# A two-layer cross-attention and expert kernel on one core: the tiles of the first expert layer that run inside the last routing chain are all put behind it

## The chip, the core and the metric

One Trainium2 chip, one of its cores, one launch. The time is microseconds (us) of device time for the whole program; lower is better. The kernel is written against the engines directly: PE (matrix multiply, with a separate row PEld for its weight loads), DVE (VectorE), ACT (ScalarE), POOL (GpSimd) and SP (SyncE, which only issues DMAs here). Each engine runs its own instruction list in the order in which it was written, and the engines wait for each other on semaphores.

## What is computed

The input is 32 batches of 128 tokens of width 128. There are two layers, each of an attention over a context and an expert network, each added to the residual:

```python
x = x + _L0_xattn_ref(_layernorm(x), ctx_768, mask, Wq, Wkv)        # 16 heads of width 8
x = x + _L0_ffn_ref(_layernorm(x), router_w, router_b, w1, b1, w2, b2)
x = x + _L1_xattn_ref(_layernorm(x), ctx_768, w_q, w_k, w_v, w_out, b_out)   # 16 heads of width 64
x = x + _L1_ffn_ref(_layernorm(x), w_router, gate_up_proj, down_proj, ...)
```

The part that matters here is the first expert network. Every token chooses its best 2 of 8 experts, and each expert takes its first 1280 arrivals in the order of the tokens:

```python
logits = xf @ router_w + router_b
topk_p, topk_i = jax.lax.top_k(softmax(logits), 2)
...                                  # rank = place of the choice inside its expert
keep = rank < cap                    # cap = 1280
buf = zeros(E * cap + 1, d).at[slot].set(xf[st])
h = gelu(einsum('ecd,edf->ecf', buf, w1) + b1)
eo = einsum('ecf,efd->ecd', h, w2) + b2
out = zeros_like(xf).at[st].add(eo_flat[slot] * w)
```

## The kernel before

**First attention.** A batch of 128 tokens is one step; four batches form a quad, and there are eight quads (0 to 7). At a quad's end its normalised rows are transposed on PE (`rows_across`, L1010, tile `gu` in, bank `of` out), copied by ACT (`take_rows`, L1499), multiplied by the router weights (`logits_front`, L960) and copied by ACT (`take_logits`, L1486). DVE picks the two best experts with a chain of small operations (`first_choice`, `second_choice`, L1771 to L1782, result `selq`). PE counts the choices (`rank_front`, L977 to L987), DVE turns the counts into row numbers (`choose_slots`, L1797 to L1806, result `slots`), and POOL scatters the quad's normalised rows into the buffer `buf` in HBM with indirect DMAs, two for each batch, so eight for a quad (`scatter_front`, L714). POOL issues them in order, and the same engine does the roots of the layer norm (`rstd_second`, L691 to L697) and one power at the end (L754).

**Tiles of the first expert network.** The buffer is worked off in 71 tiles of 128 rows (T0 to T70), expert by expert in a table that DVE makes from the counts. The first 33 (T0 to T32, `TA = 33`) hold rows of the first five quads only; their part of the table is ready before the attention ends (`list_tiles(0)`). The other 38 need the last ranks, the last scatters and the second part of the table (`cells_across(1)` on PE, L995, then `list_tiles(1)` on DVE, L1836 to L1847). The step for one tile, spread over four `body(t)` calls, is:

- SP fetches its 64 KB from `buf` into a ring of six (`fetch_tile`, L611), at most six tiles ahead of PE, and stores results with a lag of ten tiles (`store_tile`, L619). At T33 SP first writes the stores up to tile 26, then fetches.
- DVE copies the expert's first weights beside it (`stage_first`, L2235, two tiles ahead).
- PE transposes it (L1346), two tiles later makes the hidden part (L1353), four tiles later the output (L1363). ACT copies the transpose (L1660) and applies Gelu (L1666). DVE adds the bias (L2246), which lets SP store.

**Order at the end of the attention.** The last two batches, the sixth and seventh quads' logits, ranks and rows are written out by hand on PE, ACT and DVE, and between two steps of this chain stands a call that runs some tiles:

```python
output_across(LAST - 1); values(LAST);            tiles("values")
output_across(LAST);     logits_front(NQD - 2);   tiles("logits")
rank_front(NROUNDS - 2);                          tiles("ranks")
rows_across(NQD - 1);                             tiles("rows")
logits_front(NQD - 1);                            tiles("last")
rank_front(NROUNDS - 1);                          tiles("cells")
cells_across(1);                                  tiles("rest")
```

How many tiles each call takes stands in the table `ENDS` (L219), and `tiles("rest")` takes what is left and the last four bodies that drain the pipeline. ACT and DVE have the same calls at the same places. The ends of the attention's main loop on POOL and all of SP's list don't depend on the table. The second attention can start only after the 71st tile (`keys(0)` waits for `M0.y_evac`). Quads 6 and 7 are called the sixth and the last round below; their eight scatters each are called the first and the second series.

Of the kernel before, what the change touches and what calls it, by code (L numbers as in the profile page):

```python
# [215 lines left out]


SOON_TILES = {0: TA + 2 * E0, 2: TA + 4 * E0, 4: NT0}
ENDS = (("start", 2), ("values", 2), ("logits", 3), ("ranks", 1), ("rows", 1), ("last", 3), ("cells", 4))  # L219


def tiles_after(part):

    first = 0
    for name, n in ENDS:
        if name == part:
# [2152 lines left out]
```

How the kernel before makes its waits and increments, by code:

```python
def need(eng, sem, value):  # L126
    if isinstance(value, int) and value <= 0:
        return
    eng.wait_ge(sem, value)
# [361 lines left out]
            def full(self, eng, name, n):  # L492
                eng.wait_ge(self.pj_full[FILL1[name, n][0]], FILL1[name, n][1] + 1)
# [1 line left out]
            def free(self, eng, name, n):  # L495
                eng.wait_ge(self.pj_free[FILL1[name, n][0]], FILL1[name, n][1] + 1)
# [8 lines left out]
            @block.sync  # L505
# [1 line left out]
                def quad(n):  # L507
                    bs = slice(n * QH, (n + 1) * QH)
                    sp.dma_start(x[:, bs, :], a["x"][:, bs, :]).then_inc(x_in[n], 16)
                def ctx_quad(n):
                    sp.dma_start(ctxq[n % 2][:, :], a["ctxT"][:, n * QH * P:(n + 1) * QH * P])\
                        .then_inc(ctxq_in[n % 2], 16)
                quad(0)
                ctx_quad(0)
                quad(1)
                sp.wait_ge(mask_loaded, 16)
                sp.wait_ge(q_loaded, 32)
                quad(2)
                ctx_quad(1)
# [35 lines left out]
                def spread_quad(n):  # L556
                    p, us = n % 2, slice(QH * (n % 2), QH * (n % 2) + QH)
                    sp.wait_ge(j_free, J_USE["q", n] + 1)
                    if n == 1:
                        sp.wait_ge(qpad_clear, 2)
                    if n >= 2:
                        sp.wait_ge(mf_full, 2 * QH * (n - 1))
                        sp.wait_ge(sf_full, 4 * QH * (n - 1))
                    for to, src, done in ((qpadfb, qTqb, qpadfb_in), (qpadf, qTq, qpadf_in)):
```

## Time and profile before

| what | us |
|---|---|
| median of 3 runs | 972.71 (967.04 to 973.57) |
| the profiled execution | 971.4 |
| its span in the trace | 969.6 |
| first fetch of a tile, SP | 210.14 |
| last rank on PE | 244.54 |
| T32, the last early tile, on PE | 279.85 |
| T70, the last tile, on PE | 332.77 |

The profile is of one execution. Its times count from the start of the span; the stretch in question lies between 210 and 337 us. PE is the busiest engine over the whole program (860.1 us, 89%), but in this stretch it is often idle.

### The profile page before, as it was taken

The page shows a single profiled execution, that of the slowest core. Times are in us where ns is not written, and L with a number is a line of the kernel's source. Part 1 is how long each engine was busy: PE and PEld are TensorE (multiplying, and loading weights), DVE is VectorE, ACT ScalarE, POOL GpSimd, SP SyncE. Part 2 cuts the span into 40 slices and gives each one's busy share as a digit, 9 for nine tenths or more (in the row PEclk, how much of TensorE's full clock was granted, in tenths as well). Part 3 has the DMA queues.
Part 4 walks back from the last instruction along what each step waited for, and adds up shares of the span by engine and source line. Part 5 has one row for each costly group of instructions (what it writes and reads, how often), then busy time and mean ns, then how long its engine had stood idle before and what let it go on. Part 6 is the DMA issues. An engine that isn't in the chain of part 4 may idle for free.

```text
span 969.6 us, 32256 instructions
## 1 busy us (share of the span) xinstructions
PE 860.1 (89%) x12315; PEld 731.1 (75%) x12315; DVE 598.4 (62%) x1741; ACT 546.9 (56%) x1224; POOL 454.8 (47%) x545
## 2 busy tenths in 40 slices
PE   7998988986698879999999999999999987987773
PEld 3565555545687759999999999999999976867773
DVE  5887766664444466766777777777776754434441
ACT  2787766443366547666666666666666631235551
POOL 7123333364500364566556655665645434534443
PEclk7998989788699989999999999999999997999997
DMA  5345544312233316640011100110000002343320
GB/s 145 113 114 151 167 154 137 110 61 61 68 97 99 106 34 198 192 145 25 20 30 30 29 19 27 30 30 21 25 24 20 2 2 82 121 135 93 96 80 6
DMA packets 82231, 75.12 MB, mean 77 GB/s; under 512 B 14529, under 2 KB 73992, under 8 KB 81314
## 3 DMA queue, kind: packets, MB, share of 16 engines
q1 hardware_dynamic: 74146, 58.11, 20.5%
q0 software_dynamic: 7136, 14.71, 4.8%
q8 instruction: 102, 1.67, 0.8%
q14 instruction: 47, 0.39, 0.1%
q10 hardware_dynamic: 800, 0.24, 0.1%
HBM read 37.17 MB, written 34.10 MB: 73 GB/s over the span
## 4 chain that ended last, share of the span: by engine, by line
PE 72%; issue 7%; DVE 6%; ACT 5%; another core or an unknown queue 4%; DMA 2%; SPq 1%; POOL 1%; DVEq 0%; ACTq 0%; POOLq 0%
PE of L1186 7%; PE sf L1150 7%; PE jf L1080 6%; PE sf L1416 5%; PE sf L1135 5%; PE mf L1115 4%; PE jf L1089 3%; PE sf L1089 3%; PE sf L906 2%; PE of L952 2%; PE sf L1353 2%; PE sf L1272 2%; PE sf L1363 2%; PE mf L1173 2%
## 5 line engine op out<-in xcount | busy, mean ns | idle before, releaser
L775 POOL TENSOR_TENSOR pl<-pT,ph 128x512 bf16<-128x512 f32 x128 | 146.1, 1165 | 124.4 <-DVE ph L1955 123.1
L1961 DVE TENSOR_REDUCE cmxb<-mf 128x8 bf16<-128x1024 f32 x64 | 78.3, 1224 | 53.0 <-PE mf L1173 52.7
L714 POOL DMA_INDIRECT buf<-gu,slots x64 | 63.2, 987 | 99.7 <-PE of L952 70.8
L1743 DVE TENSOR_REDUCE cmx<-mf 128x8 bf16<-128x1024 f32 x64 | 78.3, 1224 | 45.7 <-PE mf L933 30.8
L764 POOL DMA_INDIRECT gb<-eo,slots x64 | 64.5, 1008 | 74.0 <-DMA eo<-rows 58.8
L1573 ACT ACTIVATE pT<-sf 128x1024 f32<-128x1024 f32 x64 | 66.9, 1045 | 26.0 <-PE sf L1156 23.8
L1480 ACT ACTIVATE pTf<-sf 128x1024 f32<-128x1024 f32 x64 | 62.5, 1021 | 31.5 <-remote 18.1
L1150 PE MATMUL sf<-qTs,kTs 64*128 64x128 f32 x1024 | 75.4, 287 | 0.0
L851 POOL DMA_INDIRECT out<-rows x47 | 45.7, 973 | 56.3 <-DVE rows L2313 46.2
L1150 PEld LDWEIGHTS sf<-qTs,kTs 64*128 64x128 f32 x1024 | 63.1, 189 | 5.7 <-issue 0.2
L1080 PE MATMUL jf<-wo,oT 128*128 128x128 f32 x480 | 60.7, 280 | 0.0
L1666 ACT ACTIVATE hT<-sf,qTs 128x128 f32<-128x128 f32 x142 | 44.6, 366 | 22.3 <-PE sf L1353 14.3
L1946 DVE TENSOR_TENSOR o1s<-of,rden 128x256 f32<-128x256 f32 x128 | 54.3, 425 | 4.4
L1080 PEld LDWEIGHTS jf<-wo,oT 128*128 128x128 f32 x480 | 56.0, 192 | 0.0
L1363 PE MATMUL sf<-dn,hT 128*128 x284 | 49.0, 301 | 7.7 <-issue 5.5
L1353 PE MATMUL sf<-qTs 128*128 128x128 f32 x284 | 49.5, 300 | 7.2 <-ACT hT L1666 5.2
L1554 ACT CAST kTb<-mf 128x512 bf16<-128x512 f32 x30 | 17.6, 586 | 65.7 <-PE sf L1115 65.7
L1115 PE MATMUL sf<-ctxT,wk 32*128 32x128 f32 x768 | 51.9, 280 | 1.1 <-ACT qTs L1544 0.7
L1135 PE MATMUL sf<-wv,ctxT 32*128 32x256 f32 x768 | 50.5, 391 | 2.5 <-DVE va10l L1970 2.5
L2305 DVE TENSOR_TENSOR hT<-kTs,sf 128x256 f32<-128x256 f32 x47 | 19.8, 421 | 52.2 <-ACT kTs L1716 49.2
L2235 DVE COPY qTs<-gu 128x258 f32 x71 | 21.1, 301 | 49.8 <-ACT hT L1666 39.6
L1416 PE MATMUL sf<-xsT,qTs 128*128 128x128 f32 x376 | 49.7, 275 | 0.0
(303 smaller groups left out, 2722.3 us busy)
## 6 DMA issues: line engine op xcount, KB each, us to landing
buf<-zero SPq DMA_DIRECT2D x12, 516.0 KB, 7.8
ctxT<-in_ctxP SPq DMA_DIRECT2D x32, 192.0 KB, 2.4
rows<-buf SPq DMA_DIRECT2D x47, 129.0 KB
buf<-zero SPq DMA_DIRECT2D x22, 256.0 KB, 3.9
eo<-zero SPq DMA_DIRECT2D x22, 256.0 KB
rows<-buf SPq DMA_DIRECT2D x71, 64.0 KB
eo<-rows SPq DMA_DIRECT2D x71, 64.0 KB, 1.6
gu<-in_gu SPq DMA_DIRECT2D x4, 1024.0 KB
```

The costliest lines, as they stand in the source:

```text
L775: nc.gpsimd.tensor_tensor(pl[h][:, :, c, :], pT[h][:, :, c, :], ph[h][:, :, c, :], ALU.subtract)\
L1080: last = nc.tensor.matmul(ps[:, 0:DM], oT[:, c, :], wo1[:, c, :], start=(c == 0), stop=(c == NCH - 1))
L1115: last = nc.tensor.matmul(banks[i][:, c * P:(c + 1) * P], wk1[rr, u, c * P:(c + 1) * P], ctxT[n % 2][rr, u, :], start=(u == 0), stop=(u == ...
L1135: last = nc.tensor.matmul(sf[:, i, 0:UC], ctxT[n % 2][rr, u, :], wv1[rr, u, :], start=(u == 0), stop=(u == CB - 1))
L1150: nc.tensor.matmul(S1[:, r, n * P:(n + 1) * P], kT[p][rr, 4 * h + n, :], qT[p][rr, 4 * h + n, :], start=(n == 0), stop=False)
L1186: last = nc.tensor.matmul(of[:, j * (D1 + 1):(j + 1) * (D1 + 1)], pp[h][:, r, n, :], va1[p][part][:, QH * g + j, :], start=(m == 0), stop= ...
L1353: last = nc.tensor.matmul(s_bank[n % 2][:, f * P:(f + 1) * P], stage0[n % DEEP][:, f * P:(f + 1) * P], xsT0[n % DEEP], start=True, stop=True)
L1363: last = nc.tensor.matmul(st_bank[n % 2][:, 0:DM], hT1[n % DEEP][:, f, :], w2r[:, bass.ds(e, 1), f, :].squeeze(1), start=(f == 0), stop=(f ...
L1416: last = nc.tensor.matmul(g_bank[n % DEEP][:, c * P:(c + 1) * P], stage[n % DEEP][:, c * P:(c + 1) * P], xsT1[n % DEEP], start=True, stop= ...
L1573: nc.scalar.activation(pT[h][:, :, :, :].rearrange("p r c n -> p r (c n)"), S1, ACT.Exp, scale=D1 ** -0.5)\
L1743: nc.vector.reduce_max(to, mf[:, :, :].rearrange("p c (j k) -> p c j k", j=QH), AX.X)\
L1961: nc.vector.reduce_max(cmx1[b % 2][:, :].rearrange("p (r k) -> p r k", r=2)[:, :, 4 * h:4 * h + 4], M1p[:, :, :].rearrange("p r (c k) -> p ...
```

## The change

The first six entries of the table go to nought; four tiles stay between the last rank and the second table.

```diff
-ENDS = (("start", 2), ("values", 2), ("logits", 3), ("ranks", 1), ("rows", 1), ("last", 3), ("cells", 4))
+ENDS = (("start", 0), ("values", 0), ("logits", 0), ("ranks", 0), ("rows", 0), ("last", 0), ("cells", 4))
```

So before, 12 bodies (T0 to T11) stand between steps of the chain and T12 to T15 in "cells"; now T0 to T3 stand in "cells" and all others in "rest".

On PE, around the ranks of the last round, the list was (the end of the "last" tiles, then the rank):

```order
L1346 MATMUL mf<-ident,rows 128x128
L1353 MATMUL sf<-qTs 128x128 x2
L1363 ISA
L1363 MATMUL sf<-dn,hT 128x128
L1363 ISA
L1363 MATMUL sf<-dn,hT 128x128
L977 MATMUL of<-selq,tri 128x32
L979 MATMUL of<-selq,ones 128x24
```

and on PE it is now, from the transposes of the last quad's rows to its ranks:

```order
L1010 MATMUL of<-ident,gu 128x128 x4
L960 MATMUL of<-rw,xrTq 128x8 x4
L977 MATMUL of<-selq,tri 128x32
L979 MATMUL of<-selq,ones 128x24
L979 MATMUL of<-selq,ones 128x16
L979 MATMUL of<-selq,ones 128x8
L980 MATMUL of<-selsum,ones 128x32
L985 MATMUL of<-selsum,ones 128x8
L987 MATMUL of<-selq,ones 128x8 x4
```

The rows, logits and ranks follow each other with no tile between them.

On ACT, around the copies of the last quad (L1451 its layer norm, L1499 the transposed rows, L1486 the logits; `hT` is a tile's Gelu, `qTs` its transpose), the difference reads:

```order
-L1666 ACTIVATE hT<-sf,qTs 128x128 x2
 L1451 ACTIVATE gu<-rows,nbb,rsb 128x128 x4
 L1499 COPY xrTq<-of 128x512
-L1660 COPY qTs<-mf 128x128
-L1666 ACTIVATE hT<-sf,qTs 128x128 x2
 L1486 COPY oh<-of 128x32
+L1660 COPY qTs<-mf 128x128 x3
```

The layer norm no longer stands behind the Gelu of tiles; the tiles' copies come after the last logits.

On DVE, ahead of the second part of the table (L1836), the difference reads (L2235 stages a tile's weights, L2246 adds a tile's output bias):

```order
-L2246 ISA
-L2246 TENSOR_TENSOR rows<-sf,dn 128x128
-L2235 ISA
-L2235 COPY qTs<-gu 128x258
-L2246 ISA
-L2246 TENSOR_TENSOR rows<-sf,dn 128x128
+L2235 ISA
+L2235 COPY qTs<-gu 128x258
 L1836 TENSOR_TENSOR oh<-of,cellc 1x400
 L1838 TENSOR_REDUCE oh<-oh 1x40
```

Before the table DVE now stages T2 to T5 and adds no bias at all, where it used to stage T14 to T17 and finish T8 to T11. SP's list and POOL's list are the same in both kernels.

## Rows read from the trace of the kernel before

**Rows 1.** The page: the chain that ended last, by engine.

```profile
PE 72%; issue 7%; DVE 6%; ACT 5%; another core or an unknown queue 4%; DMA 2%; SPq 1%; POOL 1%; DVEq 0%; ACTq 0%; POOLq 0%
```

**Rows 2.** Windows: length, busy PE, PEld, DVE, ACT, POOL, PE clock, DMA, GB/s.

```profile
220.00:231.00 11.00, 9.44 (x57) 9.03 (x57) 7.00 (x34) 6.91 (x24) 1.71 (x4) 0.69 0.13 37
231.00:241.00 10.00, 4.96 (x40) 4.55 (x40) 3.46 (x17) 2.08 (x7) 7.65 (x8) 1.00 0.30 93
...
247.00:259.00 12.00, 6.12 (x40) 5.06 (x38) 2.25 (x10) 2.11 (x8) 9.48 (x9) 0.78 0.26 81
...
283.00:337.00 54.00, 46.76 (x366) 43.71 (x367) 26.84 (x93) 35.02 (x119) 5.58 (x7) 0.97 0.36 102
```

**Rows 3.** Timeline of POOL: start, us, what, idle before it and its releaser.

```profile
198.37 0.97 POOL L714 DMA_INDIRECT buf<-gu,slots  x1 [3.51 <-PE of L952]
...
231.22 1.09 POOL L714 DMA_INDIRECT buf<-gu,slots  x1 [5.19 <-ACT gu L1451]
...
247.37 0.97 POOL L714 DMA_INDIRECT buf<-gu,slots  x1 [6.11 <-DVE slots L1806]
...
256.32 0.97 POOL L714 DMA_INDIRECT buf<-gu,slots  x1 [0.30 <-issue]
```

**Rows 4.** Timeline of ACT, the same columns.

```profile
202.78 1.94 ACT L1480 ACTIVATE pTf<-sf 128x1024 f32<-128x1024 f32 x2 [4.18 <-remote]
...
229.70 1.64 ACT L1451 ACTIVATE gu<-rows,nbb,rsb 128x128 f32<-128x128 f32 x4
...
237.02 0.19 ACT L1486 COPY oh<-of 128x32 f32<-128x32 f32 x1 [3.65 <-remote]
...
258.87 0.63 ACT L1666 ACTIVATE hT<-sf,qTs 128x128 f32<-128x128 f32 x2 [2.60 <-remote]
```

**Rows 5.** Timeline of DVE, choices, slots and table.

```profile
226.55 0.19 DVE L1782 TENSOR_TENSOR selq<-rk 128x32 bf16<-128x32 f32 x1
...
230.18 0.17 DVE L1806 TENSOR_SCALAR slots<-slotf 128x8 int32<-128x8 f32 x1
...
237.24 0.19 DVE L1771 TENSOR_TENSOR rk<-oh,rb 128x32 f32<-128x32 f32 x1 [3.21 <-ACT oh L1486]
...
240.00 0.19 DVE L1782 TENSOR_TENSOR selq<-rk 128x32 bf16<-128x32 f32 x1
...
246.34 0.17 DVE L1806 TENSOR_SCALAR slots<-slotf 128x8 int32<-128x8 f32 x1
...
260.14 0.55 DVE L1836 TENSOR_TENSOR oh<-of,cellc 1x400 f32<-1x400 f32 x1
...
262.65 0.17 DVE L1847 TENSOR_SCALAR tiles<-oh 1x40 int32<-1x40 f32 x1
```

**Rows 6.** Timeline of PE, steps of the chain.

```profile
220.83 1.11 PE L1002 MATMUL jf<-ident,oE 128*128 128x128 f32 x4 [0.15 <-ACT oE L1494]
221.74 1.71 PE L960 MATMUL of<-rw,xrTq 128*128 128x8 f32 x8
...
228.26 0.18 PE L977 MATMUL of<-selq,tri 128*128 128x32 bf16 x1
...
233.03 0.96 PE L960 MATMUL of<-rw,xrTq 128*128 128x8 f32 x8
...
244.54 0.23 PE L977 MATMUL of<-selq,tri 128*128 128x32 bf16 x1
```

**Rows 7.** Timeline of PE, transposes of T18, T24, T32, T33 and T70.

```profile
261.50 0.42 PE L1346 MATMUL mf<-ident,rows 128*128 128x128 f32 x1
...
271.49 0.30 PE L1346 MATMUL mf<-ident,rows 128*128 128x128 f32 x1
...
279.85 0.30 PE L1346 MATMUL mf<-ident,rows 128*128 128x128 f32 x1
...
283.27 0.33 PE L1346 MATMUL mf<-ident,rows 128*128 128x128 f32 x1 [2.17 <-DMA rows<-buf]
...
332.77 0.27 PE L1346 MATMUL mf<-ident,rows 128*128 128x128 f32 x1
```

## The prediction

> **What bounds the kernel now.** I read four views in this order: the chain that ended last on the page, the windows by stage, the timelines of POOL, ACT, DVE and PE from 197 to 337 us, and of those the waits that no named engine ended. The chain lies 72% on PE, with 7% "issue" and 4% "another core or an unknown queue" [rows 1]; the second of these is odd for a program on one core, and much of it lies in this stretch. The stretch from 210 to 337 us is a chain (choices, ranks, scatters) with tiles pushed into its gaps. The reader should see three things.
>
> First, while POOL issues scatters, PE's signals reach the others late. The first series of eight starts at 231.22 [rows 3]; PE has finished the last logits at 233.99 (233.03 + 0.96, rows 6), and ACT copies them only at 237.02, after 3.65 us ended by no engine [rows 4, 6]. The second series runs from 247.37 to 257.29 (256.32 + 0.97), and ACT gets going only at 258.87, again after such a wait (2.60) [rows 3, 4]. I call these holds. They are no matter of the tiles: at 202.78, before any tile was fetched, ACT waited 4.18 us in the same way, and three scatters had started at 198.37, 1.28 apart [rows 3, 4]. In the two series PE is busy for only 4.96 of 10 and 6.12 of 12 us [rows 2].
>
> Second, POOL sets the pace of the chain's end. Eight scatters take 8.95 us from first start to last start (256.32 - 247.37, or 1.28 each) and 9.92 in all [rows 3]. The second series can't begin before the first is through, whatever PE does.
>
> Third, behind the chain only tiles are left, and they set the end: T18 at 261.50, T32 at 279.85, T70 at 332.77 [rows 7], and then the second attention. Each tile not yet done when the holds end is paid in full.
>
> **What the change takes away from the chain.** Nothing is added or removed; 12 bodies move. Step by step, with the trace's durations:
>
> (a) Tiles of "start" and "values", T0 to T3. They stand in front of the copy of the last output, but that is held in any case until 220.83, when PE takes up the transposes [rows 6], by the end of the sixth quad's earlier scatters. They cost the chain nothing; taking them out gives nothing.
>
> (b) "logits", T4 to T6. The sixth round's choice is done at 226.74 (226.55 + 0.19), its rank starts on PE at 228.26 [rows 5, 6]: 1.5 us of tiles, and DVE's own tile steps add some 0.5 us more. From that rank to the slots it takes 2.1 us (230.35 - 228.26), from there to the first scatter 0.87 (231.22 - 230.35) [rows 3, 5, 6]. So the first series starts at about 229.0 instead of 231.22: 2.2 us sooner, and ends at 229.0 + 9.9 = 238.9.
>
> (c) The last quad. Its roots on POOL end some 0.5 us sooner, at 225.5, and its layer norm on ACT no longer waits behind Gelus until 229.70 [rows 4]. It then ends at 225.5 + 1.6 = 227.1; transposes 1.1 at the low clock, copy 0.6, logits 1.7 [rows 6], copies and waits 0.4: 230.9 on ACT. The choice takes 2.95 us (237.24 to 240.19) [rows 5], so the rank could start at 234 instead of 244.54 [rows 6], 10 us sooner. This is more than can be used: the second series waits for POOL, which is free at 238.9, plus the gap of 0.3 between scatters: 239.3.
>
> (d) "last", T9 to T11. The choice is done at 240.19 but the rank runs at 244.54 [rows 5, 6]: 4.35 us, as PE stands in front of tiles whose Gelu waits for held signals. This goes.
>
> So the second series starts at 239.3 at the best, 8.1 us sooner than 247.37. At the worst the holds bite in the same places, counted from the start of the series: the logits' signal comes 5.8 us after it (237.02 - 231.22), that is at 234.8, the choice ends at 237.9, and the rank's signal is held to the end of the series and 1.6 us past it (258.87 - 257.29), at 240.5; slots 1.3 us later and the scatter 0.87 after that: 242.7, which is 4.7 us sooner. **The chain gains 4.7 to 8.1 us**; I take the middle, 6.4, since nothing in the trace says which signal a hold will catch. The end of the second series and of the table move with it.
>
> **What the moved tiles cost behind it.** When DVE has written the second table (262.65 + 0.17 = 262.82), PE has done T18 (261.50) [rows 5, 7]. In the changed kernel this point comes 6.4 us sooner, at about 256.4. DVE has staged only T0 to T5 and added no bias when it comes to the table, so if the signal of the cells is held to the end of the series, PE stops after T6: 12 tiles behind. If that signal slips out before the hold begins, DVE goes on and the tiles trickle through the second series as they did before (T12 to T17 between 244.54 and 258.87), and PE stands at up to T9: 9 behind. I take 11, nearer to the first, since the list stands in the middle of a series in both kernels.
>
> The price of a tile: 1.05 us at the fast end, where SP is ahead and PE sets the pace ((279.85 - 271.49)/8), and 1.34 at the slow end, where fetch and store pace them ((332.77 - 283.27)/37) [rows 7]. SP's lead of six tiles holds only for a while, so I take 1.2: 11 x 1.2 = 13.2 us. The bounds are 9 x 1.05 = 9.4 and 12 x 1.34 = 16.1. The wait of 2.17 us at T33 [rows 7] comes from SP's own order, which is the same, and stays. No data stage is short of room: DMA is at 0.36 in the late tiles [rows 2].
>
> **Sum:** 13.2 - 6.4 = +6.8 us; from 9.4 - 8.1 = +1.3 to 16.1 - 4.7 = +11.4. Against the profiled execution's 971.4 that is 978.2. That execution lies 1.3 us under the median of the runs, 972.71, so for the median I say 979.
>
> **The clock, as a rule that speaks against the change.** PE's work in the chain is short, and it runs at either level: the same logits took 1.71 us at 221.74 and 0.96 at 233.03, with a granted clock of 0.69 over 220 to 231 us, a mean of the levels of 1.2 and 2.4 GHz, and of 1.00 from 231 to 241, when PE came from a run of tiles [rows 2, 6]. With the tiles gone the last round's transposes and logits would run at the lower level: 0.45 + 0.75 = 1.2 us more. It is in the numbers of (c), and costs nothing while the first series covers it. The Trainium skill ("TensorE: Matmul & The Clock Gate", section "What's actually happening") says that the throttled state is the default and that activity releases it. By that rule the tiles in the chain serve as warming too, and the sum would be 1.2 us higher if the rank's path, not POOL, set the second series; by the rows POOL sets it.
>
> **Rivals.**
>
> *Slower by over 1%.* The mechanism is DVE standing in front of the second table. It waits for PE's one signal of the cells; if that is held to the end of the second series, no tile is staged past T5, and all of T7 to T70 run afterwards at the slow end's pace. With the late start of the second series (242.7): 12 x 1.34 - 4.7 = +11.4, or 983 against 971.4 and 984 as a median. For it: the order on DVE, and SP's pace of 1.34. Against it: the early tiles come at 1.05 to 1.2. It decides from a price of 1.34 a tile or a gain of the chain under 5.
>
> *About even, +1 to +3.* The second series starts right behind the first (gain 8.1), the cells' signal slips out (9 tiles), and the early tiles come at PE's pace of 1.05: +1.3. Median 974.
>
> *Faster.* Holds are made by tile traffic meeting scatters, and with no tile in the chain they vanish. Then T0 starts at 234.5 and 32 more at 1.05 to 1.34 bring T32 to between 268 and 277.4, less 279.85: -2 to -12 us; with the first four at half clock about -6. Median 967. Against it stands the hold at 202.78, with no tile in flight.
>
> *The change does nothing to the order.* The lists of PE, ACT and DVE differ as meant; under 1 in 100.
>
> **How the numbers follow.** My forecast (+3.5 to +9.5) has 0.58, the slower rival 0.20, the even one 0.15, the faster one 0.06. One per cent, about what a measurement of this kernel can tell from no change, is 9.7 us. Within 1% lie the forecast, the even case and half of the faster one: 0.76; slower by over 1%: 0.21; faster by over 1%: 0.03. The range takes in the even case and the slower rival with 1 us of spread beside it: 973 to 985.
>
> **What would show it.** In the changed kernel: the first rank (L977) of the sixth round at about 226.6 and the first series at 229; the last rank between 234 and 239, with no tile in front; the second series between 239.3 and 242.7; DVE's L1836 some 6 us sooner than 260.14 unless the cells' signal slips out, when it may come at 243; T0 after the last rank; T32 near 286.7, T33 some 3.4 us later, T70 near 339.6. The stages behind the tiles should be the same to a microsecond. I would be wrong if the holds were shorter without tiles, if a series of sixteen scatters on end held longer than two of eight, or if SP, with its whole list ahead of it, paced all 71 tiles at more than 1.34.

## The result and the profile after

| | before | changed |
|---|---|---|
| median of 20 runs each, us | 974.05 (967.04 to 981.77) | 981.23 (972.68 to 987.73) |
| profiled execution: span | 969.6 | 979.4 |

The ratio of changed to before is 1.0062, 95% interval 1.0036 to 1.0087: 6.0 us slower (3.5 to 8.5); the two medians lie 7.2 us apart. A second measurement (a0 below) gave 1.0100 (1.0059 to 1.0142). Forecast was +6.8. These intervals are narrower than the doubt: in b0 below the kernel before, measured against itself, came out at 1.0054 (1.0011 to 1.0098). All ratios compare only the fast executions, those within 1.5% of a kernel's fastest, which in the set of b0, a0, e5 and e6 leaves 22 of the 35 executions of the kernel before; by the medians of all executions b0 is 2.3 us and a0 5.7 us above that kernel, e5 7.0 us and e6 3.4 us below it. So the size of the loss is known to some 0.5% of the time; its place is told by the traces.

Rows of the page of the changed kernel, span and chain by engine; the odd entry of [rows 1] is 3% here:

```profile
span 979.4 us, 32257 instructions
...
PE 72%; issue 8%; DVE 7%; ACT 5%; another core or an unknown queue 3%; SPq 2%; DMA 1%; POOL 1%; DVEq 0%; ACTq 0%; POOLq 0%
```

Two executions are not equally far when they come to this stretch: the seventh quad's transposes (L1010) are at 213.06 in the profile before and at 209.43 here, though the code up to there is the same. So all steps are counted from them. The timeline of PE, before and then changed:

```profile
213.06 0.63 PE L1010 MATMUL of<-ident,gu 128*128 128x128 f32 x4 [1.13 <-issue]
```

```profile
209.43 0.63 PE L1010 MATMUL of<-ident,gu 128*128 128x128 f32 x4 [0.99 <-ACT oE L1494]
...
218.04 1.72 PE L960 MATMUL of<-rw,xrTq 128*128 128x8 f32 x8
222.95 0.21 PE L977 MATMUL of<-selq,tri 128*128 128x32 bf16 x1 [3.19 <-DVE selq L1782]
...
225.62 1.88 PE L960 MATMUL of<-rw,xrTq 128*128 128x8 f32 x8 [0.68 <-ACT xrTq L1499]
230.80 0.21 PE L977 MATMUL of<-selq,tri 128*128 128x32 bf16 x1 [3.29 <-DVE selq L1782]
...
235.35 0.47 PE L1346 MATMUL mf<-ident,rows 128*128 128x128 f32 x1
242.50 1.20 PE L1353 MATMUL sf<-qTs 128*128 128x128 f32 x4 [6.67 <-ACT hT L1666]
...
250.67 0.42 PE L1346 MATMUL mf<-ident,rows 128*128 128x128 f32 x1
```

Each rank now waits only for DVE's choice (3.19 and 3.29 us), both logits run at the lower clock (1.72 and 1.88 us against 0.96 in [rows 6]), and PE's transposes of T4 and T6 lie 15 us apart. Here are the steps, us behind the seventh quad's transposes:

| step | before | forecast | changed |
|---|---|---|---|
| rank of the sixth round | 15.2 | 13.5 | 13.5 |
| first series of scatters | 18.2 | 15.9 | 15.9 |
| last rank | 31.5 | 21 to 26 | 21.4 |
| second series | 34.3 | 26.2 to 29.6 | 26.2 |
| second table on DVE (L1836) | 47.1 | 41 | 39.6 |
| last tile transposed by its end | T18 | T6 to T9 | T6 |
| T32 | 66.8 | 73.6 | 75.2 |
| T70 | 119.7 | 126.5 | 127.1 |
| first keys of the second attention (L1115) | 124.6 | | 132.6 |

POOL, for [rows 3]: the two series run into each other.

```profile
225.31 1.09 POOL L714 DMA_INDIRECT buf<-gu,slots  x1 [3.52 <-DVE slots L1806]
...
235.61 0.97 POOL L714 DMA_INDIRECT buf<-gu,slots  x1 [0.30 <-issue]
...
244.55 0.97 POOL L714 DMA_INDIRECT buf<-gu,slots  x1 [0.30 <-issue]
```

ACT and DVE, for [rows 4, 5]:

```profile
216.49 0.58 ACT L1494 COPY oE<-of 128x512 f32<-128x512 f32 x1 [3.17 <-remote]
...
227.54 0.18 ACT L1486 COPY oh<-of 128x32 f32<-128x32 f32 x1 [1.97 <-PE of L960]
...
241.73 0.62 ACT L1666 ACTIVATE hT<-sf,qTs 128x128 f32<-128x128 f32 x2 [7.59 <-issue]
...
248.06 0.62 ACT L1666 ACTIVATE hT<-sf,qTs 128x128 f32<-128x128 f32 x2 [3.28 <-remote]
```

```profile
231.26 0.24 DVE L1797 SCALAR_TENSOR_TENSOR lg<-of,cellc 128x80 f32<-128x80 f32 x1 [0.52 <-PE of L987]
...
242.51 0.57 DVE L2235 COPY qTs<-gu 128x258 f32 x1 [8.17 <-ACT hT L1666]
248.84 0.30 DVE L2235 COPY qTs<-gu 128x258 f32 x1 [5.75 <-ACT hT L1666]
249.05 0.56 DVE L1836 TENSOR_TENSOR oh<-of,cellc 1x400 f32<-1x400 f32 x1
```

The logits' and the last rank's signals passed without a hold this time (1.97 is the logits' own run, 0.52 the rank's). The hold came after: ACT stood still before 241.73 and again before 248.06, DVE behind it at the staging of T4 and T5, and the table followed at once. So in the changed kernel the tiles are stopped by held signals, not by DVE standing in front of the table.

Windows for [rows 2] (the same columns), the two series and the late tiles:

```profile
225.00:235.00 10.00, 5.44 (x31) 4.62 (x32) 5.31 (x26) 1.55 (x5) 7.56 (x8) 0.50 0.18 60
235.00:249.00 14.00, 3.50 (x13) 2.35 (x12) 0.73 (x2) 1.83 (x8) 11.56 (x10) 0.50 0.15 50
287.00:341.00 54.00, 47.09 (x363) 43.55 (x364) 27.10 (x93) 34.90 (x119) 5.28 (x6) 0.97 0.36 101
```

PE is busy for 3.50 of 14 us while the second series runs; the late tiles are as before. Here are the transposes of T32, T33 and T70, for [rows 7]:

```profile
284.61 0.33 PE L1346 MATMUL mf<-ident,rows 128*128 128x128 f32 x1 [0.47 <-DMA rows<-buf]
288.54 0.48 PE L1346 MATMUL mf<-ident,rows 128*128 128x128 f32 x1 [2.69 <-DMA rows<-buf]
...
336.58 0.33 PE L1346 MATMUL mf<-ident,rows 128*128 128x128 f32 x1
```

What set the pace of the tiles between the table and T32 is told by windows that begin and end at transposes. First the kernel before, T18 to T24 and T24 to T32; then the changed kernel, T6 to T12, to T18, to T24 and to T32 (columns as in [rows 2]: length, busy PE, PEld, DVE, ACT, POOL, PE clock, DMA, GB/s):

```profile
261.50:271.49 9.99, 9.05 (x55) 8.72 (x55) 5.10 (x22) 4.88 (x18) 1.27 (x1) 0.66 0.25 69
271.49:279.85 8.36, 8.36 (x74) 8.20 (x73) 4.72 (x17) 6.79 (x26) 0.00 (x0) 1.00 0.37 103
```

```profile
250.67:260.72 10.05, 9.45 (x55) 9.03 (x55) 4.60 (x20) 4.97 (x19) 0.33 (x1) 0.65 0.22 61
260.72:266.93 6.21, 6.21 (x56) 6.20 (x56) 3.38 (x12) 4.91 (x18) 0.00 (x0) 1.00 0.40 109
266.93:273.75 6.82, 6.69 (x56) 6.15 (x54) 3.60 (x13) 5.25 (x20) 0.00 (x0) 1.00 0.35 98
273.75:284.61 10.86, 9.23 (x72) 8.27 (x72) 4.75 (x17) 7.12 (x25) 0.00 (x0) 1.00 0.35 99
```

In both kernels the first six tiles behind the holds take 10.0 us, at a granted clock of 0.65 or 0.66. The next tiles take 1.04 to 1.14 us each at a clock of 1.00, with PE busy nearly all the time. Only the changed kernel's last eight are slower again, 1.36 us each: there PE waits 0.85 us and 0.47 us for rows that SP fetches.

**Why the two profiles differ by 9.8 us and not 8.** -3.6 before the stretch, +8.0 inside it (132.6 - 124.6), and +6.4 at the entry of the second attention: from its first keys to its first output projection (L1080, 377.06 before and 387.76 here) it is 39.4 us before and 45.7 here; the rest is 0.9 shorter. The entry is a hold again. ACT's first exponential there, changed kernel, beside POOL's gathers:

```profile
359.34 1.02 ACT L1573 ACTIVATE pT<-sf 128x1024 f32<-128x1024 f32 x1 [3.69 <-remote]
```

```profile
354.92 0.95 POOL L764 DMA_INDIRECT gb<-eo,slots  x1 [0.30 <-issue]
356.17 0.94 POOL L764 DMA_INDIRECT gb<-eo,slots  x1 [0.30 <-issue]
357.42 0.94 POOL L764 DMA_INDIRECT gb<-eo,slots  x1 [0.30 <-issue]
```

The order of the work there is the same in both kernels, but whether the longer entry is chance isn't shown. The kernel before took 39.4 us for it in one profile and 43.0 in another (b0), so it moves by itself; the changed kernel took 45.7 and 45.6 (a0), and e6, with ten of the twelve tiles in their old places, 45.8.

### The profile page after: what moved, and what is told of

Its sections match the earlier page's. It is cut to its first block, busy times and chain, and to the rows that moved or that the text cites. A ratio compares the mean times of both kernels' runs of the same rounds, so it can differ in the third digit from the quotient of the medians.

```text
span 979.4 us, 32257 instructions
## 1 busy us (share of the span) xinstructions
PE 855.4 (87%) x12315; PEld 726.3 (74%) x12315; DVE 600.0 (61%) x1741; ACT 547.6 (56%) x1224; POOL 454.3 (46%) x545
## 4 chain that ended last, share of the span: by engine, by line
PE 72%; issue 8%; DVE 7%; ACT 5%; another core or an unknown queue 3%; SPq 2%; DMA 1%; POOL 1%; DVEq 0%; ACTq 0%; POOLq 0%
PE of L1186 7%; PE sf L1150 7%; PE jf L1080 6%; PE sf L1416 5%; PE sf L1135 5%; PE mf L1115 4%; PE jf L1089 3%; PE sf L1089 3%; PE sf L1363 2%; PE sf L1353 2%; PE sf L906 2%; PE sf L1272 2%; PE mf L1173 2%; PE of L952 2%
## 5 line engine op out<-in xcount | busy, mean ns | idle before, releaser
L1573 ACT ACTIVATE pT<-sf 128x1024 f32<-128x1024 f32 x64 | 66.9, 1046 | 29.4 <-PE sf L1156 25.7
L1480 ACT ACTIVATE pTf<-sf 128x1024 f32<-128x1024 f32 x64 | 62.5, 1021 | 28.9 <-remote 16.4
L851 POOL DMA_INDIRECT out<-rows x47 | 45.6, 971 | 56.3 <-DVE rows L2313 46.5
L1080 PE MATMUL jf<-wo,oT 128*128 128x128 f32 x480 | 60.7, 280 | 0.0
L1080 PEld LDWEIGHTS jf<-wo,oT 128*128 128x128 f32 x480 | 56.0, 192 | 0.0
L2235 DVE COPY qTs<-gu 128x258 f32 x71 | 21.5, 305 | 54.5 <-ACT hT L1666 49.3
L1135 PE MATMUL sf<-wv,ctxT 32*128 32x256 f32 x768 | 52.6, 404 | 2.4 <-DVE va10l L1970 2.4
L1115 PE MATMUL sf<-ctxT,wk 32*128 32x128 f32 x768 | 52.8, 283 | 1.1 <-ACT qTs L1544 0.7
L1353 PEld LDWEIGHTS sf<-qTs 128*128 128x128 f32 x284 | 41.3, 209 | 10.7 <-issue 10.7
```

Of the source, the lines that this page charges most:

```text
L1080: last = nc.tensor.matmul(ps[:, 0:DM], oT[:, c, :], wo1[:, c, :], start=(c == 0), stop=(c == NCH - 1))
L1115: last = nc.tensor.matmul(banks[i][:, c * P:(c + 1) * P], wk1[rr, u, c * P:(c + 1) * P], ctxT[n % 2][rr, u, :], start=(u == 0), stop=(u == ...
L1135: last = nc.tensor.matmul(sf[:, i, 0:UC], ctxT[n % 2][rr, u, :], wv1[rr, u, :], start=(u == 0), stop=(u == CB - 1))
L1353: last = nc.tensor.matmul(s_bank[n % 2][:, f * P:(f + 1) * P], stage0[n % DEEP][:, f * P:(f + 1) * P], xsT0[n % DEEP], start=True, stop=True)
L1573: nc.scalar.activation(pT[h][:, :, :, :].rearrange("p r c n -> p r (c n)"), S1, ACT.Exp, scale=D1 ** -0.5)\
```

## The experiments

Twelve runs in three sets; in each set the kernel before ran too. The sets were not of one kind. In the second (b0, a0, e5, e6) the kernel before took 974.65 us, as on record. In the first (e1, e2, e3, e4) and the third (e7 and the three repeats) it took 886.38 and 886.24, and none of the eight traces from them has a wait of ACT, DVE or PE over 1 us that no engine ended, other than ACT's at the very start. The second and third sets ran on the same chip, so it is not the chip alone. I call them sets with and without holds.

**b0, the kernel before again** (no edit; with holds).

> The kernel before, unchanged, for a profile from the same chip as the other runs of this call; the first four runs came from a chip where it takes 886 us, not 974, and where no wait of ACT, DVE or PE over 1 us is ended by no engine. If this chip is of that kind: the last rank some 24 us behind the first transposes of the seventh quad (31.5 in the first profile), T32 some 58 us behind them (66.8). If it is of the other kind: as in the first profile.

Median 976.96 (8 runs), ratio 1.0054 (1.0011 to 1.0098) to the same kernel. The steps repeat: ranks at 15.2 and 31.6, table 47.3, T32 66.9, T70 118.6, keys 123.5. So in a set with holds a step of this stretch that moves by 2 us in one profile has moved, and a ratio under 1.005 has not been shown. Without holds the steps repeat less well: the two profiles of e4 have the last rank at 24.2 and 22.5, T32 at 49.6 and 47.3, and the keys at 107.2 and 103.1.

**a0, the changed kernel again** (no edit; with holds).

> The changed kernel, unchanged. On a chip without holds, by what the first four runs left: the last rank 17 to 18 us behind the seventh quad's transposes, T0 right behind it. Theory A (each tile left over costs 0.8 to 1.3 us, the chain gives back up to 6): +6 to +10 us against the kernel before. Theory B (without holds the chain's gaps are too short to run tiles in, so moving them costs nothing): within 3 us of it.

980.30 us, ratio 1.0100 (1.0059 to 1.0142), +9.7 us by the ratio and +5.7 by the medians of all executions. That fits theory A in size; B was about chips without holds, and the set was not one. The profile repeats the chain: ranks at 13.5 and 21.3, series at 15.8 and 26.2, table at 39.6, again with T6 as the last tile by its end. ACT again stands still twice around the second series, for 6.22 and 6.09 us, while T4 and T6 lie 15.3 us apart. T32 is at 76.0 and the keys are at 134.8, so this pair of profiles (a0 against b0) differs by 9.1 and 11.3 us where the first differs by 8.4 and 8.0.

**e5, the changed kernel without the 16 late scatters** (their rows of the buffer stay nought, and SP waits for 16 fewer; with holds), and **e4, the same cut in the kernel before** (without holds, twice).

```diff
+                    if r >= NQD - 2:
+                        return
                     nc.gpsimd.indirect_dma_start(
-                        sp.wait_ge(M0.scattered, 16 * 2 * (NB - NA))
+                        sp.wait_ge(M0.scattered, 16 * 2 * (NB - NA - 2 * QH))
```

> The changed kernel without the 16 scatters of the last two quads (their rows in the buffer stay nought). On a chip without holds: as the changed kernel, within 2 us, since then neither POOL's pace nor a signal stops the tiles (as it was for the kernel before). On a chip with holds: 10 to 20 us less than the changed kernel, and no wait ended by no engine in the chain. Rival (POOL's pace of 1.28 us a scatter bounds the second series and with it the late tiles): 4 us less on either chip.

> The kernel before without the 16 scatters of the last two quads (their rows in the buffer stay nought; everything else is done). My theory (the holds come with POOL's indirect DMAs, and they stop the tiles for some 17 us of the chain): the waits of more than 2 us ended by no engine vanish between 225 and 260 us, T32 comes at about 262 instead of 279.85, and the time falls by 14 to 20 us. Rival (the holds have another cause, code loading or the tiles' own DMAs, and only POOL's pace goes): the waits stay, and the time falls by 5 us or less.

> The kernel before without the 16 scatters of the last two quads, for a second time (-1 us on the chip without holds). On a chip with holds: no wait ended by no engine in the chain after the first, T32 at 50 instead of 66.8, and 12 to 18 us less than the kernel before. With the changed kernel's -14.8 for the same cut this gives what the move costs without late scatters. Rival (only POOL's pace goes): 5 us less or fewer.

e5: 967.62 us, ratio 0.9948 (0.9916 to 0.9979), against 980.30 for the changed kernel in the same set: 12.7 us less by the medians, 14.8 by the ratios. PE's timeline of e5 (its lines are 2 higher, its seventh quad is at 213.00):

```profile
234.31 0.21 PE L979 MATMUL of<-selq,tri 128*128 128x32 bf16 x1 [3.27 <-DVE selq L1784]
...
238.87 0.47 PE L1348 MATMUL mf<-ident,rows 128*128 128x128 f32 x1
...
240.85 0.29 PE L1348 MATMUL mf<-ident,rows 128*128 128x128 f32 x1
...
241.87 0.27 PE L1348 MATMUL mf<-ident,rows 128*128 128x128 f32 x1
```

The rank and T4 stand where they stood (21.3 and 25.9), but T6 comes 3.0 us behind T4 instead of 15.3, at 28.9 instead of 41.2. The hold of 12.3 us is gone, and with it about the same in time. The rival's 4 us is outside what was measured. The wait over 1 us that no engine ended nearest to the chain is ACT's of 4.28 us at 7.1, while earlier scatters still run.

The expectation of e4 names another cause for the holds, the loading of code. The changed kernel's trace speaks against it: the DMA view of 230 to 253 us, in which ACT stands still for 7.59 and 3.28 us, lists the queues of POOL's and of SP's transfers and no instruction queue.

```profile
DMA packets 1136, 1.16 MB, mean 50 GB/s; under 512 B 288, under 2 KB 928, under 8 KB 1136
## 3 DMA queue, kind: packets, MB, share of 16 engines
q0 software_dynamic: 416, 0.83, 10.5%
q1 hardware_dynamic: 720, 0.33, 5.0%
```

e4: 886.35 and 887.62 us, ratios 0.9989 (0.9956 to 1.0022) and 1.0004 (0.9977 to 1.0030). Both times the set had no holds, and the cut was worth nothing that can be told. The first expectation, 14 to 20 us with no condition, failed; the second, 12 to 18 us on a chip with holds, was not tested. The rival allowed 5 us or less, and its own price, POOL's pace, isn't seen either. Taken together, and with the caution that e5 and e4 are cuts in two different kernels, late scatters cost 13 to 15 us where holds are and nothing that shows where they are not. What e4 would give with holds wasn't measured.

**e1, T0 to T3 back between the last outputs** (edit against the changed kernel; without holds, twice).

```diff
-ENDS = (("start", 0), ("values", 0), ("logits", 0), ("ranks", 0), ("rows", 0), ("last", 0), ("cells", 4))
+ENDS = (("start", 2), ("values", 2), ("logits", 0), ("ranks", 0), ("rows", 0), ("last", 0), ("cells", 4))
```

> T0 to T3 go back between the last outputs of the attention (start 2, values 2); the other eight tiles stay behind the last ranks. My theory (these four ran inside a hold and cost the chain nothing; each tile left over costs about 1.3 us behind the chain): the first series, the last rank and the second series come as early as in the changed kernel, PE stands at T10 instead of T6 when DVE writes the second table, T32 comes some 5 us sooner than in the changed kernel, and the time is 1 us above the kernel before (-2 to +3). Rival (the four tiles delay the last output and with it the chain): the chain loses 2 to 4 us again, and the time is as in the changed kernel, +5 to +7.

> Start 2, values 2, cells 4, nothing else, for a second time (+6.6 us on the chip without holds, where T0 to T3 pushed the first rank from 8.3 to 10.5 us). On a chip with holds, by my theory T0 to T3 run inside a hold and are free: first rank at 13.5, table at 39.6, PE at T10 there, T32 at 70 to 71, +3 us against the kernel before. Rival (they cost the chain there too): first rank at 15 or later, +7 us.

894.15 and 896.58 us: 1.0074 (1.0048 to 1.0100) and 1.0088 (1.0055 to 1.0121), +6.6 and +7.8. The expected +1 failed. Without a hold these four are not free: the sixth round's rank stands 10.5 and 10.3 us behind the seventh quad's transposes, against 8.3 in both profiles of e3, which has no tile there. That is 2.1 us of chain. The first profiles of e1 and of e3, the seventh quad's transposes and the sixth round's rank:

```profile
188.08 0.63 PE L1010 MATMUL of<-ident,gu 128*128 128x128 f32 x4
...
198.58 0.21 PE L977 MATMUL of<-selq,tri 128*128 128x32 bf16 x1 [4.20 <-DVE selq L1782]
```

```profile
192.92 0.63 PE L1010 MATMUL of<-ident,gu 128*128 128x128 f32 x4
...
201.21 0.21 PE L977 MATMUL of<-selq,tri 128*128 128x32 bf16 x1 [3.55 <-DVE selq L1782]
```

What the second expectation says of a chip with holds stays untested.

**e2, only T0 to T3 taken out** (edit against the kernel before; without holds).

```diff
-ENDS = (("start", 2), ("values", 2), ("logits", 3), ("ranks", 1), ("rows", 1), ("last", 3), ("cells", 4))
+ENDS = (("start", 0), ("values", 0), ("logits", 3), ("ranks", 1), ("rows", 1), ("last", 3), ("cells", 4))
```

> The complement: T0 to T3 are taken from start and values, the other entries keep their numbers (3, 1, 1, 3), so the chain holds eight tiles as before. My theory: the chain is as late as in the kernel before (last rank some 16 us behind the first), nothing is gained, and four tiles are left over: +5 us (+3 to +7). Rival (the loss is made by the tiles of logits to last, not by the number left over): +0 to +2.

889.56 us, 1.0017 (0.9990 to 1.0044): no difference can be told. My +5 (+3 to +7) failed, and the rival's 0 to +2 holds its figure: four tiles left over did not cost four times 1.3 us. They gave some 2 us back to the chain, as e1 shows, and the last rank came 12.8 us behind the first instead of the 16 that I had taken from the profile with holds. What became of the rest is not shown.

**e3, twelve tiles in front of the second table** (edit against the changed kernel; without holds, twice).

```diff
-ENDS = (("start", 0), ("values", 0), ("logits", 0), ("ranks", 0), ("rows", 0), ("last", 0), ("cells", 4))
+ENDS = (("start", 0), ("values", 0), ("logits", 0), ("ranks", 0), ("rows", 0), ("last", 0), ("cells", 12))
```

> As the changed kernel, but 12 tiles instead of 4 stand between the last rank and the second table, so DVE stages T2 to T13 and adds biases before it stands in front of the table. My theory (held signals stop the tiles in the second series, not DVE): PE gets to T6 or T8 by the end of the second series as before, the table comes later than 252 without harm, and the time is +6 against the kernel before (+4 to +8). Rival (DVE's place in front of the second table stops the tiles): PE stands at T9 or further, and the time is +2 or less.

> Twelve tiles in cells, for a second time (+4.8 us on the chip without holds). On a chip with holds, theory (held signals stop the tiles): T6 at 40 to 42 as in the changed kernel, +7 to +10. Rival (DVE before the table stops them): T6 before 35, +2 or less.

891.97 and 890.07 us: 1.0054 (1.0026 to 1.0083) and 1.0058 (1.0029 to 1.0087), +4.8 and +5.1, inside the first range but without the hold that it argued from. Its mechanism isn't borne out: PE had done T12 by the end of the second series, where I had said T6 or T8 and the rival T9 or further. Here DVE's place may matter a little: from T6 to T12 it takes 6.5 and 6.6 us, against 8.0 and 8.2 in e1, where the table (2.7 us of DVE) falls between them; but e1 and e3 differ in four more tiles, so this is argued. The twelve tiles behind the ranks in this kernel are worse than twelve between the chain's steps by 5 us, with no hold in play.

**e6, the two tiles of ranks and rows taken out** (edit against the kernel before; with holds).

```diff
-ENDS = (("start", 2), ("values", 2), ("logits", 3), ("ranks", 1), ("rows", 1), ("last", 3), ("cells", 4))
+ENDS = (("start", 2), ("values", 2), ("logits", 3), ("ranks", 0), ("rows", 0), ("last", 3), ("cells", 4))
```

> Tiles stay where PE waits for a choice on DVE or for the last outputs (start 2, values 2, logits 3, last 3, cells 4); the two of ranks and rows, which stand in front of the last quad's layer norm, transposes and logits, go behind the last ranks. By theory A the chain gains 1 to 2 us from them and two more tiles are left, 1.6 to 2.6 us: 0 to +1.5 us against the kernel before. Rival (those two delay the last quad's layer norm on ACT by their Gelus, 3 to 4 us): -2 us.

971.22 us, 0.9973 (0.9935 to 1.0011): 2.6 us less by the ratio, at the rival's -2 and below my 0 to +1.5, but not shown to be faster. Its trace bears on (d) of the prediction, the 4.35 us that the rank stood behind the tiles of "last". PE and DVE around the last rank:

```profile
237.10 0.18 PE L977 MATMUL of<-selq,tri 128*128 128x32 bf16 x1
```

```profile
241.71 0.30 DVE L2235 COPY qTs<-gu 128x258 f32 x1 [5.41 <-issue]
243.39 0.30 DVE L2235 COPY qTs<-gu 128x258 f32 x1 [0.57 <-ACT hT L1666]
243.81 0.23 DVE L1797 SCALAR_TENSOR_TENSOR lg<-of,cellc 128x80 f32<-128x80 f32 x1
```

PE had the last rank 24.2 us behind the seventh quad (7.3 sooner than before), but DVE took it up only at 243.81, 6.7 us later, since it stood at the staging steps of the three tiles of "last", which wait for held Gelus. The second series came at 33.2, only 1.1 sooner than before. So (d) was half the story: PE's place in front of the tiles held the rank up, and DVE's would have done so without it.

**e7, tiles only where PE waits in any case** (edit against the kernel before; without holds).

```diff
-ENDS = (("start", 2), ("values", 2), ("logits", 3), ("ranks", 1), ("rows", 1), ("last", 3), ("cells", 4))
+ENDS = (("start", 2), ("values", 2), ("logits", 0), ("ranks", 0), ("rows", 0), ("last", 3), ("cells", 4))
```

> Start 2, values 2, last 3, cells 4; logits, ranks and rows take none. Seven tiles in the chain instead of twelve, at the places where PE waits anyway. On a chip with holds, by my theory as it now stands (the chain can end 7.5 us sooner; a tile left over costs 1.3 us; T0 to T3 are free): first series 15.9, last rank 21.4 to 22.5, second series 26.2, second table 39.6 us behind the seventh quad's transposes, PE at T13 there, T32 at 65 (66.8 in the kernel before), -1 to -3 us. On a chip without holds: the table as early, but with no hold to hide T0 to T3: +2 to +4 us. Rival (the choice of where is noise, what counts is the number left over): five tiles left, +4 to +6 on either.

889.94 us, 1.0035 (1.0010 to 1.0060), +3.1 us (0.9 to 5.3), in the range given for a set without holds; the interval takes in the low end of the rival's +4 to +6 too, and by b0 such a ratio isn't shown to differ from 1. The table came at 26.2 with PE at T13, T32 at 51.4. Whether it beats the kernel before with holds wasn't measured; no version here that does all the work is shown to beat it.

## Why the prediction was right, step by step

**Direction and size.** +6.8 was forecast; +6.0 (3.5 to 8.5) and +9.7 were measured, and +8.0 and +11.3 in the stretch itself, in two pairs of profiles. The changed kernel's median of 981.23 lies in the range of 973 to 985.

**(a), T0 to T3 cost the chain nothing.** True in the traces with holds: the last output's copy on ACT is 7.1 us behind the seventh quad's transposes in both kernels (220.19 - 213.06, 216.49 - 209.43). PE's logits behind it start at 8.7 and 8.6. It was stated as a fact of the kernel, and it goes with the hold: without holds they cost 2.1 us (e1 against e3).

**(b), 2.2 us on the first series.** 18.2 to 15.9: 2.3. Its own parts, 1.5 and 0.5, make 2.0.

**(c) and (d), a gain of 4.7 to 8.1, taken as 6.4.** It was 8.1 at the second series (34.3 to 26.2) and 7.5 at the table. The best end came true because the rank left PE 5.5 us behind the start of the first series and its signal passed. The reasoning that POOL, not the chain's path, sets the second series is shown by [0.30 <-issue] at 235.61. At the lower clock the last round's transposes took 1.09 us (0.66 before) and its logits 1.88 (0.96 before), 1.35 us more where 1.2 was said, and POOL covered it. (d) is less sure than it was written: see e6.

**"While POOL issues scatters, PE's signals reach the others late."** Not always, even in a set with holds. In both profiles of the changed kernel five scatters of the first series start before the last rank's signal reaches DVE, and the chain has no hold up to there. No tile runs in that time and SP moves no data; the holds begin once T0 to T4 run, in the middle of the run of sixteen. So the best end of the chain's gain came from something that the prediction couldn't say.

**The moved tiles, 11 at 1.2 = 13.2 us.** This is the term that was too small. PE stood at T6, so 12 were left, and from T6 to T32 a tile took (284.61 - 250.67)/26 = 1.31 us: 12 x 1.31 = 15.7, less 7.5, is 8.2, and T32 came 8.4 later. The price could have been read from [rows 7]: from T18 to T32 the kernel before takes (279.85 - 261.50)/14 = 1.31 us as well, and 1.05 was read from its last eight tiles alone. The mechanism given for the slow end, fetch and store, isn't what made it so: over these 26 tiles PE is busy for 31.6 of 33.9 us. Both kernels pay once for six tiles at the lower clock. What the changed kernel has on top is twelve tiles in 13.0 us (T12 to T24, 1.09 each), and 2.5 us more on the last eight, where SP's lead runs out; together 15.5. The cost was forecast 2.5 us too small and the gain 1.1 too small. That the sum was off by 1.4 only is luck in this measure: the two errors stand against each other.

**The stages behind the tiles, the same to a microsecond.** They were not: the entry of the second attention was 6.4 us longer, and why is open.

**The rivals.** The slower one's mechanism, DVE in front of the table, is not what stopped the tiles with holds (DVE waited 8.17 and 5.75 us at the staging, and not at the table), though its 12 tiles came true. The faster one, holds made by tile traffic meeting scatters, fell by its result, since the holds came back as soon as tiles ran beside scatters. Its mechanism isn't refuted for this stretch: the chain without tiles had no hold (1.97 and 0.52), and e5, with tiles and no late scatters, has none either. But tiles aren't needed for a hold, as 4.18 us at 202.78 [rows 4], 3.17 us at 216.49 above and 3.69 us beside the gathers show. No run parts the two. The even case fell with its 1.05 a tile and its 9 tiles.

**Left open.** The changed kernel itself was never run in a set without holds, and of the kernel before no profile was taken in one. The nearest runs, e3 and e1, were 4.8 to 7.8 us slower there, so a loss of that size may be argued for, but it isn't measured. Nor does one price a tile fit all runs: with 2, 4, 5, 8 and 12 tiles left over, e6, e2, e7, e1 and e3 came out at -2.6, +1.5, +3.1, about +7 and +5 us (e6 with holds, the others without). And it isn't known what makes a set one with holds; e1, e3 and e7, the three that would have parted place and number there, fell in sets without.

## What to carry to other kernels

Work that fills a dependent chain's gaps should be priced by what the chain gains when it goes and by the pace at which the same work runs behind it; here 7.5 us against 12 tiles at 1.31, the same 1.31 that these tiles had taken behind the chain before the change. Place a filler behind the step on which the chain waits, on every engine's list: three tiles that cost PE nothing kept DVE from the last rank for 6.7 us (e6). And count steps from a landmark just ahead of the change: with holds these repeated to 0.2 us up to the second table, in both kernels, where whole runs of one kernel spread by 1.5%. At T32 the changed kernel's two profiles already differ by 0.8 us.

## What the runs showed of the hardware that was not expected

With POOL's indirect DMAs in flight, PE's signals reached ACT and DVE 2 to 8 us late: 4.18 us with three scatters in [rows 4], 7.59 us in the changed kernel within a run of sixteen. In the six traces with holds, all 138 waits of over 2 us that no engine ended (after the first 20 us) had an indirect DMA of POOL starting within them or at most 1.3 us before; an instruction load started in or up to 1 us before 53 of them. Taking sixteen scatters away took 12.3 us off the time between T4 and T6. In other sets the same DMAs, issued 1.28 us apart, held nothing, and the whole program was 88 us shorter (974.65 against 886.24 on one chip). ACT's timeline of the second run of e1, without holds, in the midst of its sixteen scatters (200.51 to 220.83):

```profile
208.31 0.62 ACT L1666 ACTIVATE hT<-sf,qTs 128x128 f32<-128x128 f32 x2 [0.61 <-PE sf L1353]
209.37 0.27 ACT L1660 COPY qTs<-mf 128x128 f32<-128x128 f32 x1 [0.44 <-PE mf L1346]
210.23 0.62 ACT L1666 ACTIVATE hT<-sf,qTs 128x128 f32<-128x128 f32 x2 [0.59 <-PE sf L1353]
```

The cause of the holds is not shown. Where they exist, the late scatters bring the late ones on (e5), but scatters alone don't always make one: five of the changed kernel's first series had started before any hold came.
